# The opening pair of layers 1 to 3: the next pair's G product behind the transposes of the rows, and H's two parts ahead of G's copies and sum

## The reference

```python
def _layer(x, style, w, b, mw, mb, typ):
    s = style @ mw.T + mb
    weight = SCALE * w * s[:, None, :, None]
    demod = lax.rsqrt(jnp.sum(weight * weight, axis=(2, 3)) + EPS)
    weight = weight * demod[:, :, None, None]
    ...  # 'same': conv of 3 taps; 'upsample': transposed conv, blur; 'downsample': blur, conv of stride 2
out = x
for i, typ in enumerate(('same', 'upsample', 'same', 'downsample')):
    out = _layer(out, style, weights[i], biases[i], mod_w[i], mod_b[i], typ)
```

## Time and profile before

| | us |
|---|---|
| median of 3 runs | 2137.48 (2134.39 to 2138.97) |
| profiled execution | 2135.69, its span 2133.9 |
| PE busy | 1992.6 (93%) |
| DVE busy | 1151.5 (54%) |
| ACT busy | 916.3 (43%) |
| POOL busy | 370.8 (17%) |
| DMA, mean over the span | 104 GB/s |

### The profile page before, as it was taken

One profiled execution on the slowest core, in us unless ns is written; L12 is line 12 of the kernel. 1 busy time (PEld: TensorE's weight loads), 2 busy tenths in 40 slices (PEclk: granted clock), 3 DMA queues, 4 the chain that ended last, 5 costly groups with the idle time before them and its releaser, 6 DMA issues. The chain is left out here.

```text
span 2133.9 us, 30322 instructions
## 1 busy us (share of the span) xinstructions
PE 1992.6 (93%) x9768; PEld 1663.3 (78%) x9768; DVE 1151.5 (54%) x1987; ACT 916.3 (43%) x1395; POOL 370.8 (17%) x457
## 2 busy tenths in 40 slices
PE   4899968799999989999899999998999999999999
PEld 3677733788999977887788888877888878878886
DVE  5888888654554445336644444446555433343333
ACT  4477754444444322003433333324666544433442
POOL 4122211211111110002111111112212122222221
PEclk9899989899999999999999999998999999999999
DMA  7566646322211144444211111114333211132114
GB/s 178 183 178 186 182 145 232 131 69 72 66 59 59 59 141 138 147 138 146 96 59 59 59 59 59 59 50 125 104 102 105 92 47 52 44 135 94 52 44 162
DMA packets 118606, 222.27 MB, mean 104 GB/s; under 512 B 18336, under 2 KB 65184, under 8 KB 117792
## 3 DMA queue, kind: packets, MB, share of 16 engines
q1 hardware_dynamic: 102048, 212.36, 31.6%
q10 hardware_dynamic: 16512, 9.31, 1.6%
HBM read 159.04 MB, written 62.59 MB: 104 GB/s over the span
## 5 line engine op out<-in xcount | busy, mean ns | idle before, releaser
L1009 PE MATMUL ps<-l_u_hi,l_g_hi 128*128 128x512 f32 x512 | 210.8, 412 | 21.0 <-DVE l_u_lo L1375 10.3
L1194 ACT ACTIVATE rows<-ps,l_EY,dem3e 128x512 f32<-128x512 f32 x128 | 99.1, 778 | 278.3 <-PE ps L1009 260.5
L1009 PE MATMUL ps<-l_u_lo,l_g_hi 128*128 128x512 f32 x512 | 205.8, 402 | 0.0
L1009 PE MATMUL ps<-l_u_hi,l_g_lo 128*128 128x512 f32 x512 | 205.6, 402 | 0.0
L123 POOL TENSOR_TENSOR rows<-l_EY,ones 128x4 f32<-128x4 f32 x128 | 36.3, 284 | 807.7 <-ACT rows L1194 807.7
L2391 DVE SCALAR_TENSOR_TENSOR f_prod<-ps,b,f_gate 128x512 f32<-128x512 f32 (+1 forms) x88 | 66.0, 750 | 172.2 <-ACT f_gate L2331 172.2
L2432 POOL TENSOR_TENSOR x_lo<-f_prod,x_hi 128x512 fp32r<-128x512 f32 (+1 forms) x88 | 104.9, 1192 | 289.7 <-ACT x_hi L2338 289.7
L1375 DVE SCALAR_TENSOR_TENSOR l_u_lo<-ps,s_u,l_u_hi 128x512 fp32r<-128x512 f32 x128 | 95.2, 748 | 84.7 <-ACT l_u_hi L1176 83.7
L1176 ACT ACTIVATE l_u_hi<-ps,s_u 128x512 fp32r<-128x512 f32 x128 | 87.9, 689 | 122.3 <-PE ps L952 74.2
L2261 PE MATMUL ps<-pt_hi,v_hi 128*128 128x512 f32 (+1 forms) x352 | 138.7, 394 | 1.7 <-PEq L594 1.7
L2261 PE MATMUL ps<-pt_lo,v_hi 128*128 128x512 f32 (+1 forms) x352 | 138.3, 393 | 0.0
(11 more groups left out here) (347 smaller groups left out, 5009.7 us busy)
## 6 DMA issues: line engine op xcount, KB each, us to landing
x<-rows SPq DMA_DIRECT2D x64, 512.0 KB, 2.9
xin<-x SPq DMA_DIRECT2D x96, 256.0 KB, 4.0
rows<-x SPq DMA_DIRECT2D x48, 512.0 KB, 4.3
out<-rows SPq DMA_DIRECT2D x32, 512.0 KB, 2.6
v<-in_ffn_v SPq DMA_DIRECT2D x84, 128.0 KB, 2.6
xin<-in_x SPq DMA_DIRECT2D x16, 512.0 KB, 5.4
xb<-in_x SPq DMA_DIRECT2D x16, 512.0 KB, 3.2
x<-xb SPq DMA_DIRECT2D x16, 512.0 KB, 2.6
```

The costliest lines, as they stand in the source:

```text
L1009: mm = nc.tensor.matmul(ps[:, 3 + h, :], Gs[ws][:, h, at:at + P], Us[ms][:, h, 1 + q:1 + q + HALF], start=(k == 0), stop=(k == 11))
L1194: nc.scalar.activation(hs[:, h, :], ps[:, 3 + h, :], ACT.Identity, bias=EY[:, 1, 0, bass.ds(h * NP + p, 1)], scale=dem3e[:, bass.ds(h * NP ...
```

## The change

In layers 1, 2 and 3, opening pair only:

- TensorE: `weights_g(1)` stands behind `transpose_h(0)` instead of ahead of it. Both stay behind `edges_y` and ahead of `ffn(0)`.
- ScalarE: H's high part and two chunks, then G's two copies and high part. Before: G's copies, a chunk, H's high part, a chunk, G's high part.
- VectorE: H's low part, a chunk, then G's sum and low part. Before: G's sum, a chunk, H's low part, G's low part.

Layer 0 keeps its order.

```diff
@@ TensorE, iteration, first @@
                     edges_y()
-                    weights_g(1)
+                    if layer == 0:
+                        weights_g(1)
                     transpose_h(0)
+                    if layer > 0:
+                        weights_g(1)
                     if layer > 0:
                         ffn(0, ahead)
@@ ScalarE, first_pair @@
                 read_h(0, 0)
                 read_h(0, 1)
+                if layer > 0:
+                    split_h(0)
+                    some_chunks(2)
                 cross_g(1)
-                if layer > 0:
-                    some_chunks(1)
-                else:
-                    split_g(1)
-                split_h(0)
-                if layer > 0:
-                    some_chunks(1)
-                    split_g(1)
+                split_g(1)
+                if layer == 0:
+                    split_h(0)
                 some_chunks(len(chunks))
@@ VectorE, first_pair @@
+                if layer > 0:
+                    split_h(0)
+                    some_chunks(1)
                 sum_g(1)
                 if layer == 0:
                     split_g(1)
-                some_chunks(1)
-                split_h(0)
-                if layer == 0:
+                    some_chunks(1)
+                    split_h(0)
```

## The result

The changed kernel takes 2144.49 us, the median of 7 runs (2141.89 to 2147.9), against 2136.06 for the kernel before (7 runs, 2129.91 to 2138.97): a ratio of 1.0042, 95% interval 1.0031 to 1.0053. It is slower by about 9 us where 2.4 was forecast. Its profiled execution is one of the 7, 2144.49 us with a span of 2142.7.

A forecast was written before the change was run, and what follows sets the result against it. TensorE, by far the busiest engine, was taken as the bound, so delays ahead of its running parts are not made up. 1.56 + 1.52 - 0.66 = +2.4 us gave a median of 2139.9; range 2136.5 to 2143.5.

The forecast's parts named there:

- Who waits for what: Opening pairs: ffn(0) in layers 1 and 2 waits for G's sum, which ends last; layer 3 has no such wait.
- the two holes of layer 1: TensorE idle in layer 1: some 2.2 us ahead of the transposes and 3.4 between G and ffn(0).
- the hole ahead of main: Layer 3, between ffn(0) and main of pair 1: a new wait of 1.4 to 2.8 us for G's low part.
- Layers 1 and 2, the start of ffn(0): ffn(0) starts at 413.59 instead of 412.03 and 1027.88 instead of 1026.36: losses of 1.56 and 1.52 us.
- I leave their end at 407.58 and cost it at nothing: Layer 1's transposes: the last four wait for GpSimd's second patch, so their end stays at 407.58, at no cost.
- a sign of being wrong: The prediction would be wrong if the transposes' end moved by more than 0.3.
- Layer 3, main of pair 1: Main of pair 1 starts at 1487.57 instead of 1488.23, a gain of 0.66 us.
- The clock: Restarts in layers 1 to 3: full clock returns equally long after restart, so all delay counts; bounds -0.5 to +7.6.
- rival B: Layers 1 to 3: holes lower the clock, 1.7 us each time; +4.1 once, +5.8 twice, +7.5 three times; chance 0.20.
- Nothing for the cover of the gate product: Layer 2: gate product 2.5 us later, its use 1.5 later, 0.8 us of cover left, so no cost.

The follow-up runs named there:

- no_chunk_fill: Against before, TensorE's order kept: layers 1, 2 chunks behind G's copies, sum and H's parts; layer 3 H first; useless products behind the transposes: 2130.39 us, 0.9977.
- the second trace: The changed kernel once more, unchanged, with a second set of 11 runs: 2142.09 us, 1.0028 of the kernel before.
- before_again: The kernel before once more, unchanged, for a second trace of it: 2135.76 us, ratio 0.9994.
- Fill: The changed kernel plus eight useless products between G and ffn(0) in layers 1 and 2, and between ffn(0) and main in layer 3: 2137.91 us, 1.0009 of before.
- late_wait: The changed kernel with layer 2's wait for G's sum moved behind the small products into bank 7: 2143.00 us, 1.0037 of before.

## Why the prediction was wrong

The direction and the places were right, the size was not: +2.4 forecast, 6 to 9 measured. Term by term, the measured ones against before from the two traces of the changed kernel:

- *Who waits for what.* Right. In layers 1 and 2 ffn(0) starts with the sum, H's low part lies ready 3.9 us, the two holes of layer 1 are 2.00 and 3.53 (forecast 2.2 and 3.4), layer 3 has the hole ahead of main.
- *Layers 1 and 2, the start of ffn(0)*, forecast +1.56 and +1.52: mis-sized, +2.11 and +2.13, +2.08 and +2.17. The step "I leave their end at 407.58 and cost it at nothing" failed: it moved by 0.4, beyond the 0.3 that the prediction had set as a sign of being wrong. Without G in front of them the transposes ran at the lower clock: from the second patch's end at 406.66 + 0.77 = 407.43 to G at 408.25, 0.8 us for four, where four took 0.41 at the full level (1017.53 to 1017.94 in no_chunk_fill). That is 0.4; two chunks took 2.02 and not 1.90, for another 0.1.
- *Layer 3, main of pair 1*, forecast -0.66: -0.21, and -0.62 in the second trace. Mis-sized in the first trace: G's copies began 0.3 later than forecast, behind the slow transposes, and main started 0.25 after G's low part and not 0.05. In the second trace the forecast holds.
- *The clock*, the step of the sum that failed most: I took its loss as equal before and after, and left the hole ahead of main in layer 3 without a price. There rival B's mechanism is what happened: in all four traces with that order the level fell within main of pair 1, and from main of pair 1 to main of pair 2 it cost 1.5 us each time (+1.49 in both of the changed kernel, +0.06 in before_again). The hole there was 2.3 to 2.5 us, in the forecast range of 1.4 to 2.8, and I gave B 0.20. Fill, which in layer 3 shortens this hole alone, took the fall away and the loss with it. In layer 2 the return took 6.2 and 5.8 us after the restart where before it took 4.7 (4.1 in before_again), for another 0.5 to 0.7; in layer 1 it took 3.0 in one trace and gave 0.7 back, and 4.8 in the other, as before. No run here shows why it comes later in layer 2.
- *Nothing for the cover of the gate product*: right in the changed kernel (it ended at 1040.74, TensorE used it at 1042.60), which leaves the 1.8 us of cover that it had before and not the forecast 0.8. In late_wait, where ffn(0) starts 3.7 sooner, this product is what is late.

The sum of the openings, 1.8 + 3.1 + 1.3 = 6.2 us, agrees with the second set of runs (5.9); that closely is luck, given the 1 us or so that the sum is good to. It is more than the terms above add up to in layer 2 (2.1 and 0.6), since before_again's opening there was 0.9 shorter than before's. The 8.4 us of the first set are not accounted for. B with one or two stretches, +4.1 to +5.8, was the nearest case. The range's upper end, 2143.5, was 1 us below the median.

```profile
1017.53 0.66 PE L1023 MATMUL ps<-ident,rows 128*128 128x128 f32 x4 [0.48 <-POOL rows L123]
1017.94 2.10 PE L973 MATMUL ps<-c_hi 128*128 128x512 f32 x8
```

These two rows of no_chunk_fill are the ones for the transposes at the full level.

## What to carry to other kernels

Before an order is changed to bring one operand sooner, list every wait of the consumer: the one moved back may be the one that ends last, and work put ahead of it in an in-order engine (two chunks, 1.8 us) counts in full. Opening a new idle stretch of 2.3 to 2.5 us ahead of wide products was paid in TensorE's clock (1.5 us) as well as in waiting. A restart's price in clock is no constant to cancel against the old one: where the order had changed, the full level came back up to some 2 us sooner or later after the restart. Where an expected total is met, check that its parts are. Compare two traces of the kernel before first: here parts that the change never touched differ by 4 us between them.

## What the runs showed of the hardware

- The eight 128x128 float32 transposes take twice as long at the lower clock: 0.20 us each from start to start (0.80 for four) against 0.10.
- The lower level came after a hole of 2.3 to 2.5 us ahead of main of pair 1 in layer 3 (four traces of four), whose products have 512 columns, and not where eight products of no use shortened it to 0.63 us, nor after a hole of 1.29 us in the same place in no_chunk_fill.
- Where ffn(0) restarts at the lower level, the full one came back 2.8 to 6.0 us after the restart in layer 1 and 3.9 to 6.6 in layer 2. Where the order there is that of before, it took 4.6 to 4.9 and 4.1 to 4.7 (three traces); where the order had changed, anything in these ranges. Half of such a difference is time: up to 1.6 us an opening.
- Eight such products, 1.97 us, in a hole of 3.9 us kept the full level up to a restart 1.92 us later; with them the changed kernel's openings of layers 1 and 2 were 1.3 to 2.2 us shorter.
- A step of the router's chain, 128x8 elements, took 2.21 us in the changed kernel's layer 2, where its like take 0.17. GpSimd's add of the bias ran beside it, from 1035.41 to 1037.81, and the step ended at 1037.83. In all twelve traces one such step of the chain is long (1.7 to 2.4 us), not always the same one, and in all twelve it ends 0.02 to 0.03 us after this add. So VectorE's step is held until GpSimd's is done, as far as coincidence in twelve traces can show it; no run took the add away. The step lies in the path of the gate product, and so holds it back by 1.5 to 2.2 us in every version.

```profile
1035.41 2.40 POOL L1733 TENSOR_TENSOR rows<-rows,l_bias 128x1024 f32<-128x1024 f32 x1 [13.37 <-DMA rows<-x]
1035.62 2.21 DVE L1529 TENSOR_TENSOR l_logit<-l_small,l_router_bias 128x8 f32<-128x8 f32 x1
...
1040.45 0.29 DVE L1547 TENSOR_TENSOR l_hg<-l_small,l_gate 128x128 f32<-128x128 f32 x1
```
